# Edge stage of a graph kernel: two products stay in their PSUM banks through mish

## The reference, cut to what matters

```python
def mish(x):
    return x * jnp.tanh(jax.nn.softplus(x))
x = mish(node_features @ W_dense.T + b_dense)
y = mish(edge_features @ W_edge.T + b_edge)      # 106250 x 256
msg = jax.nn.relu(x[src] + y)
agg = jax.ops.segment_sum(msg, dst, num_segments=node_features.shape[0])
rst = x + agg
return mish(rst @ W_out.T + b_out)
```

## Time and profile before

| | us |
|---|---|
| runs, median of 3 | 4262.16 (4260.17 to 4264.4) |
| profiled execution | 4256.23 |
| its span, first to last instruction | 4254.5 |

### The profile page before, as it was taken

How to read it: one execution, slowest core, us unless ns; L and a number is a source line. 1 busy time by engine, 2 the same in 40 slices (tenths; PEclk the granted TensorE clock), 3 DMA queues, 4 the chain that set the end, 5 groups by cost and what they waited for, 6 DMA issues and landing times. The chain is left out here.

```text
span 4254.5 us, 68494 instructions
## 1 busy us (share of the span) xinstructions
PE 3499.8 (82%) x17723; PEld 3081.8 (72%) x17723; DVE 2292.7 (54%) x7003; ACT 1939.1 (46%) x3024; POOL 2806.6 (66%) x2732
## 2 busy tenths in 40 slices
PE   5777777877747999999999968888887887649999
PEld 5666666666636888888888867777777777538887
DVE  5566656565543455555445436666666666632222
ACT  4555555555531333333333445555555555423333
POOL 3677777777767777766666137777777777354334
PEclk8888888888867999999999977777777777559999
DMA  5555555555552222222222136666666666544443
GB/s 145 177 187 184 176 180 178 184 177 178 179 166 57 65 66 72 65 63 68 65 64 64 31 113 214 205 209 209 209 209 202 214 210 187 172 142 88 97 99 60
DMA packets 275818, 599.12 MB, mean 141 GB/s; under 512 B 61759, under 2 KB 150558, under 8 KB 275499
## 3 DMA queue, kind: packets, MB, share of 16 engines
q1 hardware_dynamic: 153243, 334.71, 24.4%
q0 software_dynamic: 115808, 248.88, 21.8%
q10 hardware_dynamic: 6576, 13.36, 0.9%
HBM read 460.33 MB, written 138.24 MB: 141 GB/s over the span
## 5 line engine op out<-in xcount | busy, mean ns | idle before, releaser
L1656 POOL DMA_INDIRECT y_node<-node_table,src_sb x832 | 850.8, 1023 | 382.5 <-issue 380.6
L494 POOL DMA_INDIRECT conv_gath<-support_table,src_sb x832 | 875.9, 1053 | 269.2 <-issue 256.3
L1096 POOL DMA_INDIRECT x_gath<-hidden_table,src_sb x832 | 795.4, 956 | 361.8 <-issue 260.1
L649 PE MATMUL conv_pz<-conv_we,conv_edge 128*128 128x256 f32 x2240 | 631.0, 445 | 69.8 <-PEq L97 69.7
L1669 PE MATMUL y_pa<-y_hot,y_node 128*128 128x64 f32 x3328 | 518.1, 323 | 192.8 <-PEq L97 192.1
L1669 PEld LDWEIGHTS y_pa<-y_hot,y_node 128*128 128x128 f32 x3328 | 500.9, 237 | 226.0 <-issue 223.1
L649 PEld LDWEIGHTS conv_pz<-conv_we,conv_edge 128*128 128x128 f32 x2240 | 502.0, 230 | 159.6 <-issue 74.4
L640 PE MATMUL conv_ps<-conv_hot,conv_gath 128*128 128x64 f32 x1664 | 258.0, 307 | 214.4 <-DMA conv_gath<-support_table,src_sb 212.2
L640 PEld LDWEIGHTS conv_ps<-conv_hot,conv_gath 128*128 128x128 f32 x1664 | 244.9, 221 | 247.0 <-DMA conv_gath<-support_table,src_sb 240.1
L1721 ACT ACTIVATE y_node<-y_node 128x1024 f32<-128x1024 f32 x208 | 219.3, 1055 | 344.2 <-ACTq L97 343.6
L1679 PE MATMUL y_pz<-y_we,y_edge 128*128 128x256 f32 x1104 | 360.8, 498 | 11.9 <-PEq L97 11.9
(11 more groups left out here) (257 smaller groups left out, 5817.2 us busy)
## 6 DMA issues: line engine op xcount, KB each, us to landing
conv_edge<-in_edge_t SPq DMA_DIRECT2D x140, 512.0 KB
edge_mish_table<-conv_neg SPq DMA_DIRECT2D x140, 512.0 KB
y_neg<-edge_mish_table SPq DMA_DIRECT2D x139, 512.0 KB, 4.1
y_edge<-in_edge_t SPq DMA_DIRECT2D x69, 512.0 KB
e_rows<-expert_rows SPq DMA_DIRECT2D x56, 272.0 KB, 3.4
conv_gath<-support_table,src_sb POOLq DMA_INDIRECT x832
x_gath<-hidden_table,src_sb POOLq DMA_INDIRECT x832
y_node<-node_table,src_sb POOLq DMA_INDIRECT x832
```

The costliest lines, as they stand in the source:

```text
L494: pool.indirect_dma_start(gath[g % SLOTS][:, j, :], None, table[:, :], bass.IndirectOffsetOnAxis(ap=c.src[:, col:col + 1], axis=0),).then_ ...
L649: last = pe.matmul(ps_z[r % 2][:, j, :], edge[r][:, m, j * P:(j + 1) * P], we[:, m, :], start=m == 0, stop=m == KD - 1)
L1096: pool.indirect_dma_start(gath[g % SLOTS][:, j, :], None, table[:, :], bass.IndirectOffsetOnAxis(ap=c.src[:, col:col + 1], axis=0),).then_ ...
L1656: pool.indirect_dma_start(node[g % SLOTS][:, j, :], None, c.t3[:, :], bass.IndirectOffsetOnAxis(ap=c.src[:, col:col + 1], axis=0),).then_i ...
```

## The change

Only `stage_edges` is changed. The bias is added to the product in place, in `ps_z[r]`. The minimum q is made from `ps_z[r]`, and the last step of mish reads its second input from `ps_z[r]` and writes to `z[r]` in SBUF as before. `z_free[r]` is given after the last step in place of after the bias add. In the output path, the subtraction from `xo` is made in two instructions of 256 columns in place of one of 512.

```diff
             def mish_begin(r):
                 take(dve, z_done[r])
                 dve.sem_inc(edge_free[r], 1)
-                link(dve, nc.vector.tensor_tensor(z[r][:], ps_z[r][:], bias[:].unsqueeze(1).to_broadcast([P, CG, D]), ALU.add), own)
-                dve.sem_inc(z_free[r], 1)
-                nc.vector.tensor_scalar(q[r][:], z[r][:], ZMAX, None, ALU.min).then_inc(z_ready[r], 1)
+                here = ps_z[r][:]
+                link(dve, nc.vector.tensor_tensor(here, here, bias[:].unsqueeze(1).to_broadcast([P, CG, D]), ALU.add), own)
+                nc.vector.tensor_scalar(q[r][:], here, ZMAX, None, ALU.min).then_inc(z_ready[r], 1)
 
             def mish_end(r):
                 take(dve, q_ready[r])
-                link(dve, nc.vector.scalar_tensor_tensor(z[r][:], q[r][:], -1.0, z[r][:], ALU.add, ALU.mult), own)
+                link(dve, nc.vector.scalar_tensor_tensor(z[r][:], q[r][:], -1.0, ps_z[r][:], ALU.add, ALU.mult), own)
+                dve.sem_inc(z_free[r], 1)
...
             def output_end(b=0, to=ps_o, w=PART):
-                now, x = qo[b][0:w, :, :], xo[b][0:w, :, :]
+                now = qo[b][0:w, :, :]
                 take(dve, fo_ready)
                 link(dve, nc.vector.scalar_tensor_tensor(now, now, -1.0, to[0:w, 0:2, :], ALU.add, ALU.mult), own)
                 if to is ps_o:
                     dve.sem_inc(o_free, 1)
                 take(dve, xo_in[b], 16)
-                link(dve, nc.vector.tensor_tensor(x, x, now, ALU.subtract), own)
+                for half in range(2):
+                    x = xo[b][0:w, half, :]
+                    last = nc.vector.tensor_tensor(x, x, qo[b][0:w, half, :], ALU.subtract)
+                link(dve, last, own)
                 dve.sem_inc(xo_ready, 1)
```

## The result

The changed kernel takes 4219.6 us (median of 4 runs, 4216.8 to 4221.9) against 4261.2 for the kernel before beside it. The ratio is 0.9901, 95% interval 0.9885 to 0.9917: 1% faster, some 42 us. Four further runs, made beside the experiments, gave 4215.8 and a ratio of 0.9891 (0.9875 to 0.9907).

What follows compares the result with a forecast made beforehand. POOL's back-to-back gathers were taken to bound the stage, with DVE's +38 us hidden in its waits. Last step -28.1, minimum -14.0 and halves -3.8 gave -45.9 us from 4262.2: 4216.3 us, range 4205 to 4238.

Steps and rivals of the forecast that it cites:

- The bound: In stage_edges: POOL's stream of 832 gathers, 1104.0 us, sets the stage, not landings or DVE's added time.
- Steps 1 and 2: In mish: reading PSUM, the last step frees 28.1 us of longer gathers and the minimum frees 14.0 us.
- Price of the minimum: In mish: the minimum from PSUM takes 1224 ns in place of 709, +35.5 us of DVE.
- Step 4: Output subtraction in two halves: longer gathers cost 1.2 us in place of 5.0, DVE works 2.5 us more.
- Step 5: z_free given after the last step of mish: banks stay taken longer, but PE never waits for them.
- The short adds: Message adds L1791: they keep their 17 us of longer gathers; as a bound 35 us, +18.
- The cover: DVE's 151.0 us of waits for gathered rows hide its +38 us of work, leaving 67 us of wait.
- first rival: Last step of mish: two SBUF inputs don't stop gathers, so only the minimum's 14.0 us go: 4248; chance 0.05.

Runs made afterwards that it cites:

- e1: Kernel before with only the last step of mish changed, its second input read from PSUM (product without bias): 4226.6 us against 4264.0, ratio 0.9908.
- e2: Kernel before with only the minimum reading PSUM (product without bias) and the bank given after the last step: 4249.3 us, ratio 0.9970.
- e5: Changed kernel plus one unused 1024-column DVE add per iteration, both inputs in SBUF: 4238.8 us, ratio to the kernel before 0.9937.
- e6: Changed kernel plus the same added step as e5, but with its first input from PSUM: 4222.8 us, ratio to the kernel before 0.9902.
- e3: Kernel before with only the output's subtraction in two instructions of 256 columns: 4265.2 us, ratio 0.9999.
- e7: Changed kernel plus the added step of e6 behind the last step of mish for both r: 4233.6 us, ratio to the kernel before 0.9930.
- e9_pieces: Kernel before with only the last step of mish cut into four pieces of 256 columns, both inputs still in SBUF: 4239.9 us, ratio 0.9941.
- e10: Changed kernel with some message adds reading PSUM, plus the convolution stage's last mish step in four pieces: 4188.5 us, ratio to the kernel before 0.9818.
- e12: e10 with the convolution stage's double-rate minimum in four pieces too: 4220.8 us, ratio to the kernel before 0.9896.

## Why the prediction was right, point by point

- **The bound.** Right. POOL issues without pause before and after; the stream fell by 43.3 us, the runs by 42 and 48. So neither landings nor DVE's added time set the stage. In the profiled pair the span fell by only 36.8, since the stage began 3.5 us later and the stages behind it took 3 us more. Such differences of some microseconds between executions are the noise in which every part here is measured.
- **Steps 1 and 2, last step and minimum.** Right in size: 28.1 and 14.0 went to 0 and 0, and e1, e2, e5 and e6 show the mechanism. Wrong in one thing that the sum didn't notice: the two terms aren't independent. 8 us of the minimum's 14 were caused by the phase that the last step's stops imposed, so the last step alone was worth 36 to 37.
- **Price of the minimum.** 1225 ns where L1771 gave 1224; 35.5 us expected, 35.6 in the groups.
- **Step 4, the halves.** 5.0 us of stops became 0.2 in the changed kernel, where I had 1.2, and 1.5 in e3, which has the halves alone. By time they can't be told from nothing.
- **Step 5, the longer hold.** Right: PE waits ahead of no product but the first.
- **The short adds.** This is what the sum missed. I held them at 17 us in all; with the one-hot step they took 20.7. 47.1 us of stops were there to go (28.1, 14.0, 5.0), 0.2 stayed, and 4 came back in the short steps: 43 in all. The bound that I gave for this (35 us) covers it. In e2 and e5 they took 25 us each, so this is the term that moves with every edit.
- **The cover.** 67 us of wait expected, 70.0 measured. e7 shows where it ends.
- **A row that I read wrongly.** For the first rival I counted 42 gathers that "needed their early part" in L1781 and paid 0.7 us. 28 of them had an L1781 that started at most 0.025 us ahead of them. In these traces two inputs didn't stop a gather when the step started at the same time or later. The first adds of the messages give the border. In before, after and e9_pieces none that starts less than 0.03 us ahead of a gather stops it, and every one that starts 0.05 to 0.25 ahead does. Between, e9_pieces has three that stop one (0.032, 0.039, 0.047), and before and e9_pieces have some at 0.033 and 0.034 that don't. So that rival had nothing on its side, and a chance of 0.05 was too much for it.

## What to carry to other kernels

Where POOL issues indirect DMAs back to back and sets the pace, look first at where DVE's steps read and only then at how long they take. Here the steps that read two SBUF tiles added to the gathers that began inside them (28.1 us for 69 last steps, 10.6 for the 34 added in e5), and so did the double-rate minima (14.0 us for 69). The minimum that reads PSUM takes 73% longer (1225 ns against 709), and the kernel with it was 15 us faster (e2). If a step must read SBUF twice, cut it into short pieces: in e9 the stops fell from 28.1 to 5.4 us, in e10 the gathers' busy time from 875.2 to 832.3. For the double-rate minimum this didn't pay (e12, 32 us slower than e10). Then count DVE's slack, for both remedies can cost DVE time, and once its waits were used up POOL waited for DVE, 11.5 us in e7 and 93.8 in e12. All of this was measured with float32 tiles and gathers of 128 rows.

## What the runs showed of the hardware that I had not expected

- What a step's stops cost depended on the phase between the two engines, and other stops fixed that phase: 9.2 us of late stops behind an untouched minimum became 0.9 in e1_last, when the last step ceased to stop gathers.
- In before, after and e9_pieces, a short add with two inputs in SBUF (0.42 us) that started less than 0.03 us ahead of a gather, or after it, didn't stop it; each one that started 0.05 to 0.25 us ahead did. Of the steps here only the double-rate minimum has a late point as well, 0.12 us before a gather's end: in before 42 gathers paid there for 9.2 us.
- A double-rate minimum cut in four costs 309 ns a piece for a quarter of 709.
